# A graph layer by counts: the first layer's sum over edges as a product of an edge-count matrix and the node table, run in three stretches per block

## The reference, cut to what matters

```
t1    = feat @ W1
msg   = (t1[src] + feat[src] * feat[dst] @ W2) / (sqrt(deg[src]) * sqrt(deg[dst]))
agg   = segment_sum(msg, dst)
embed = l2_normalize(leaky_relu(t1 + agg + b))
```

## Time and profile before

| what | value |
|---|---|
| time, median of 3 runs | 5443.28 us (5443.25 to 5448.71) |
| profiled execution, span | 5537.5 us |
| mean granted TensorE clock | 0.835 of full |
| PE busy | 3805.9 us (69%) |
| DVE busy | 3132.6 us (57%) |
| ACT busy | 1618.8 us (29%) |
| POOL busy | 3849.2 us (70%) |
| DMA | 572.85 MB, mean 103 GB/s |

### The profile page before, as it was taken

One profiled execution on the slowest core, in us unless ns is written; L12 is line 12 of the kernel. 1 busy time (PEld: TensorE's weight loads), 2 busy tenths in 40 slices (PEclk: granted clock), 3 DMA queues, 4 the chain that ended last, 5 costly groups with the idle time before them and its releaser, 6 DMA issues.

```text
span 5537.5 us, 68744 instructions
## 1 busy us (share of the span) xinstructions
PE 3805.9 (69%) x19471; PEld 2905.8 (52%) x19471; DVE 3132.6 (57%) x12068; ACT 1618.8 (29%) x6417; POOL 3849.2 (70%) x4302
## 2 busy tenths in 40 slices
PE   6555555555556555555557887888788888888886
PEld 6444444444444444444445665656566666665654
DVE  8756565665655656555555555555455555555545
ACT  3144444544444444444420111111111111111111
POOL 0177776777777777776757777777777777777772
PEclk9577777777777777777779989999999998999988
DMA  4333333333333333333334444444444444444443
GB/s 97 117 94 97 93 99 92 99 94 98 98 97 96 96 98 93 96 95 94 95 104 116 113 111 111 113 115 112 110 115 110 115 114 110 111 110 114 112 108 76
DMA packets 278430, 572.85 MB, mean 103 GB/s; under 512 B 88622, under 2 KB 167790, under 8 KB 278056
## 3 DMA queue, kind: packets, MB, share of 16 engines
q0 software_dynamic: 164640, 456.82, 31.9%
q1 hardware_dynamic: 101576, 103.13, 6.9%
q10 hardware_dynamic: 11840, 8.50, 0.5%
HBM read 541.27 MB, written 26.92 MB: 103 GB/s over the span
## 4 chain that ended last, share of the span: by engine, by line
PE 42%; DVE 31%; another core or an unknown queue 16%; issue 9%; DMA 1%; ACT 0%; SPq 0%; DVEq 0%; PEldq 0%; ACTq 0%
PE psE L736 18%; DVE both L1366 8%; PE psY L717 6%; PE psT L717 6%; DVE work L1453 5%; DVE work L1449 4%; PE psE L936 3%; PE psE L917 3%; DVE work L1293 2%; PE psY L693 1%; DVE work L1383 1%; DMA acc_d<-work 1%; DVE work L1374 1%; PE psE L872 1%
## 5 line engine op out<-in xcount | busy, mean ns | idle before, releaser
L630 POOL DMA_INDIRECT work<-t_d,srci x3430 | 3271.3, 954 | 1587.8 <-issue 1155.8
L736 PE MATMUL psE<-work,both 128*128 128x257 f32 x6860 | 2219.4, 448 | 875.8 <-issue 373.7
L736 PEld LDWEIGHTS psE<-work,both 128*128 128x128 f32 x6860 | 1388.0, 225 | 1242.5 <-issue 469.2
L1109 ACT ACTIVATE work<-work 128x35 f16<-128x35 bf16 x5145 | 1133.5, 311 | 692.0 <-DVE work L1449 440.9
L1366 DVE TENSOR_SCALAR both<-iof,dstf 128x128 f32<-128x128 f32 x3430 | 813.7, 345 | 47.8 <-issue 25.7
L1449 DVE TENSOR_SCALAR work<-iob,work 128x35 bf16<-128x35 bf16 x1715 | 273.3, 269 | 806.4 <-remote 668.9
L1383 DVE TENSOR_TENSOR work<-work,psY 128x257 f32<-128x257 f32 x857 | 347.5, 420 | 631.1 <-PE psY L717 206.5
L1383 DVE TENSOR_TENSOR work<-work,psT 128x257 f32<-128x257 f32 x858 | 348.0, 420 | 601.1 <-PE psT L717 214.6
L717 PE MATMUL psT<-relb,work 126*128 126x257 bf16 x2574 | 452.1, 286 | 21.2 <-DVE work L1374 19.1
L717 PE MATMUL psY<-relb,work 126*128 126x257 bf16 x2577 | 459.8, 290 | 0.5 <-issue 0.5
L627 POOL MEMSET work<- 128x640 bf16 x571 | 380.2, 666 | 0.2
(11 more groups left out here) (262 smaller groups left out, 3291.1 us busy)
## 6 DMA issues: line engine op xcount, KB each, us to landing
work<-t_d,srci POOLq DMA_INDIRECT x3430
work<-types_d SPq DMA_DIRECT2D x245, 220.5 KB
both<-acc_d SPq DMA_DIRECT2D x98, 130.0 KB
t_d<-accf SPq DMA_DIRECT2D x7, 910.0 KB, 9.3
acc_d<-work ACTq DMA_DIRECT2D x1, 6370.0 KB
t_d<-accf SPq DMA_DIRECT2D x49, 130.0 KB
X<-in_x SPq DMA_DIRECT2D x1, 6144.0 KB
out<-X SPq DMA_DIRECT2D x6, 896.0 KB
```

Of the source, the lines that this page charges most:

```text
L630: pool.indirect_dma_start(gath[:, n % RG, :], None, table, bass.IndirectOffsetOnAxis(ap=srci[:, n:n + 1], axis=0)).then_inc(s_g[n % RG], 16)
L736: ins = nc.tensor.matmul(psE[:, b % 2, 0:DW], sel[:, third, k % SG, :], gath[:, n % RG, 0:DW], start=False, stop=(k == C - 1))
L1109: ins = nc.scalar.activation(to_s3[:, n % 2, i, j, :], to_s[:, n % 2, i, :], ACT.Copy, scale=load3[:, b // RB % 2, j, w:w + 1])
```

## The change

The first layer's sum no longer gathers rows. For each block of 128 targets it builds the matrix of edge counts, 6272 sources by 128 targets, and multiplies it with the whole table, which stays in SBUF as three bf16 parts that add up to the f32 value. In parts:

1. *Windows.* Each block is cut in 16 windows of 8 nodes (784 in all, `STEPS`). For each window SP loads 3x128 targets and sources at an address from a register (`windows`: 32 small transfers a block), ACT turns them to floats, TensorE transposes them (`turn_window`).
2. *One-hots.* For four windows at a time the Vector engine makes the one-hots with `tensor_tensor` over rows whose innermost run is four 16-bit values (`edge_hots`); `sends` is rewritten in the same form and takes over the scaling that ACT did.
3. *Histogram steps.* Each window is three bf16 products, 392, 294 and 147 columns wide, into one PSUM bank (two banks in turn), and ACT copies the 392 counts to bf16 (`counts_out`).
4. *Counts times table.* 49 sources x 3 parts = 147 bf16 products a block (`collect`), a block later, in three runs of 48, 48 and 51 at steps 5, 10 and 15.
5. *Start.* The table's three parts are made in SBUF; `t1_d` and a zeroed `acc_d` are still written for the fallback of unsorted inputs. X is loaded again block by block in the first pass, stored to `x1_d`, and all of it is loaded back at the start of the second pass, ahead of the third load of types. All seven `parts` now stand behind the last step.
6. GpSimd issues nothing in the first pass. The second pass is the same.

The fallback is taken where a block or window has more edges than its room. In the diff the loop over `range(STEPS + 50)` is TensorE's and the one over `range(STEPS + 55)` the Vector engine's; `at(t, lag)` gives the block whose step 0 lies `lag` steps back.

```diff
+NODES = 8
+WINS = P // NODES
+TAKE = 3
+REACH = ((0, 8), (2, 8), (5, 8))
+FOUR = 4
+STEPS = NB * WINS
...
+            def windows(b):
+                if b >= 2:
+                    sp.wait_ge(s_wtp, b - 1)
+                sp.load(firsts, start_w[0:1, WINS * b:WINS * b + WINS])
+                for w in range(WINS):
+                    first = sp.snap(firsts[w], min_val=0, max_val=E)
+                    for r, a in enumerate((dst_p, src_p)):
+                        sp.dma_start(ints[TAKE * w:TAKE * w + TAKE, b % 2, r, :],
+                                     a[bass.ds(first, ROOMY)].rearrange("(p e) -> p e", e=P)).then_inc(s_wl[b % 2], 16)
...
+            for b in range(NB + 3):
+                if b + 2 < NB:
+                    windows(b + 2)
+                if b >= 3:
+                    store_row(b - 3)
+                if b < NB:
+                    load_x(b)
                 if b + 1 < NB:
-                    load_old(0, b + 1)
+                    load_old0(b + 1)
...
+                for c in {NB - 1: (0, 1), NB: (2, 3), NB + 1: (4, 5), NB + 2: (6,)}.get(b, ()):
+                    load_pair(c)
...
+            load_types(0)
+            load_types(1)
+            for c in range(NB // 7):
+                sp.dma_start(X[:, 7 * c:7 * c + 7, :],
+                             x1_d.rearrange("(b p) d -> p b d", p=P)[:, 7 * c:7 * c + 7, :]).then_inc(s_xl, 16)
             sp.dma_start(f1, w1.rearrange("(t p) n -> p t n", p=P)).then_inc(s_fw, 16)
             sp.dma_start(f2, w2.rearrange("(t p) n -> p t n", p=P)).then_inc(s_fw, 16)
...
+            def histogram(t):
+                n, j = t // FOUR, t % FOUR
+                bank = (psT, psY)[t % 2][:, 1, :]
+                if j == 0:
+                    pe.wait_ge(s_r, n + 1)
+                if t >= 2:
+                    pe.wait_ge(s_a, t - 1)
+                for c, (lo, hi) in enumerate(REACH):
+                    ins = nc.tensor.matmul(bank[:, lo * NB:hi * NB], hot_l[n % 2][:, c, :, j],
+                                           hot_r[n % 2][:, AT[c]:AT[c + 1], j], start=(c == 0), stop=(c == TAKE - 1))
+                ins.then_inc(s_h, 1)
+
+            def collect(b, w):
...
+                for s in sources(w):
+                    for part, (at0, wide) in enumerate(((0, DW), (DW + 1, D), (DW + 1 + D, D))):
+                        ins = nc.tensor.matmul(bank[:, 0:wide], adj[:, b % 2, s, :], parts_t[:, s, at0:at0 + wide],
+                                               start=False, stop=(s == NB - 1 and part == 2))
...
+                for t in range(STEPS + 50):
+                    b, w = t // WINS, t % WINS
+                    if t < STEPS:
+                        histogram(t)
+                    if 1 <= b <= NB and w >= 1:
+                        collect(b - 1, w)
+                    if b + 1 < NB and w == 6:
+                        turn_window(b + 1)
+                    if b < NB and w in (4, 9, 14):
+                        move(b, w // 5)
...
+                    for m in at(t, 49):
                         feed_forward(m)
...
+                    for m in at(t, 46):
                         turn_ffn(m)
...
+                    for m in at(t, 37):
                         messages(m)
...
+                    for m in at(t, 35):
                         turn_features(m)
...
+            def counts_out(t):
+                b, w = t // WINS, t % WINS
+                if w == 0 and b >= 2:
+                    act.wait_ge(s_agg, b - 1)
+                act.wait_ge(s_h, t + 1)
+                bank = (psT, psY)[t % 2][:, 1, :]
+                nc.scalar.copy(adj[:, b % 2, :, NODES * w:NODES * w + NODES],
+                               bank[:, 0:NODES * NB].rearrange("p (d s) -> p s d", s=NB)).then_inc(s_a, 1)
...
+            def edge_hots(n):
+                b, j = n // FOUR, n % FOUR
+                if n >= 2:
+                    dve.wait_ge(s_h, FOUR * (n - 1))
+                mine = slice(FOUR * j, FOUR * j + FOUR)
+                for c, (lo, hi) in enumerate(REACH):
+                    many = (hi - lo) * NB
+                    v.tensor_tensor(hot_r[n % 2][:, AT[c]:AT[c + 1], :],
+                                    keyed_hi[:, b % 2, c, mine].unsqueeze(1).broadcast_to([P, many, FOUR]),
+                                    ramp[:, lo * NB:hi * NB, :], ALU.is_equal)
+                v.tensor_tensor(hot_l[n % 2][:, :, :, :],
+                                keyed_lo[:, b % 2, :, mine].unsqueeze(2).broadcast_to([P, TAKE, P, FOUR]),
+                                ramp[:, 0:P, :].unsqueeze(1).broadcast_to([P, TAKE, P, FOUR]), ALU.is_equal).then_inc(s_r, 1)
...
             def sends(b, g):                          # one third of a block: 12 columns
...
+                link(v.tensor_tensor(to_s, four(spot_s[:, r % 2, i, some]).broadcast_to([P, THIRDS, C, FOUR]), count(C),
+                                     ALU.is_equal))
+                for j in range(3):
+                    v.tensor_tensor(to_s3[:, n % 2, :, j, :, :], to_s,
+                                    four(load3[:, r % 2, j, i, some]).broadcast_to([P, THIRDS, C, FOUR]), ALU.mult)
+                v.tensor_tensor(to_q[:, n % 2, :, :, :], four(spot_q[:, r % 2, i, some]).broadcast_to([P, THIRDS, P, FOUR]),
+                                count(P), ALU.is_equal).then_inc(s_tq, 1)
...
+                for t in range(STEPS + 55):
+                    if t % FOUR == 0 and t // FOUR + 1 < BATCHES:
+                        edge_hots(t // FOUR + 1)
+                    if b < NB and w in (1, 6, 11):
+                        sends(b, w // 5)
...
+                    for m in at(t, 54):
+                        table_row(m)
+                    for m in at(t, 51):
+                        fed(m)
+                    for m in at(t, 45):
+                        ffn_input(m)
+                    for m in at(t, 42):
+                        residual(m)
+                    for m in at(t, 39):
+                        embeddings(m)
+                    for m in at(t, 33):
+                        features(m)
```

More of the change, by code:

```diff
@@ L34 @@
 RG = 18
-BURST = [6, 3]
+BURST = 3
+NODES = 8
+WINS = P // NODES
+TAKE = 3
+REACH = ((0, 8), (2, 8), (5, 8))
+ROOMY = TAKE * P
+FOUR = 4
+BATCHES = NB * WINS // FOUR
+STEPS = NB * WINS
+AT = [sum(hi - lo for lo, hi in REACH[:c]) * NB for c in range(TAKE + 1)]
+TW = 3 * D + 2
+XR = 3
+THIRDS = 3
+HALF = -(-NB // 2)
+TC4 = 12
+ENOUGH = ((2, 7.0), (5, 16.0), (8, 24.0))
+MOST = 16.0
 MM = 6
@@ new lines, in program @@
+        q = o - 8 * W
+        grown = arena[:, q:q + STEPS].rearrange("p (b u) -> p b u", u=WINS)
+        q += STEPS
+        ended = arena[:, q:q + NB]
+        q += NB
+        below = arena[:, q:q + NB]
+        q += NB
+        bands = arena[:, q:q + P].rearrange("p (k u) -> p k u", k=4)
+        q += P
+        offset = arena[:, q:q + WINS]
+        q += WINS
+        inside = arena[:, q:q + WINS]
+        q += WINS
+        under = arena[:, q:q + WINS]
+        q += WINS
+        over = arena[:, q:q + NB]
@@ L401, in program @@
         s_scaled = sem("s_scaled")
-        s_td = sem("s_td")
+        s_td = [sem(f"s_td{k}") for k in range(2)]
         s_sel = sem("s_sel")
@@ L568, in _ @@
+            sp.wait_ge(s_part, NB)
             unordered(0)
[L569 to L573 removed]
+            load_old0(0)
+            for b in range(NB + 3):
[5 more added lines that the diff above has]
+                    load_x(b)
@@ new lines, in rank_tri, with move @@
+            def rank_tri(b):
+                pe.wait_ge(s_pl, 2 * b + 1)
+                mine = marked[:, b % RB, :, :].rearrange("p c k -> p (c k)")
+                nc.tensor.matmul(psT[:, 0, 0:BINS * C], trib[:, :], mine, start=True, stop=True).then_inc(s_rp, 1)
+            def move(b, g):
+                n = THIRDS * b + g
+                pe.wait_ge(s_tq, n + 1)
+                if g == 0 and b >= 1:
+                    pe.wait_ge(s_so, b)
+                for k in third(g):
+                    i, t = k % TC4 // FOUR, k % FOUR
+                    ins = nc.tensor.matmul(psY[:, 0, 0:3 * C], to_q[:, n % 2, i, :, t], to_s3[:, n % 2, i, :, :, t],
+                                           start=(k == 0), stop=(k == C - 1))
+                ins.then_inc(s_sm, 1)
@@ L1083, in _ @@
[L1083 to L1096 removed]
+            act.wait_ge(s_padd, 64)
@@ new lines, in _ @@
+            for n in range(EN):
+                if n >= 2:
+                    dve.wait_ge(s_hmm, n - 1)
+                for one_hot, bits, wide in ((ohlo, end_lo, P), (ohhi, end_hi, NB)):
+                    ins = v.tensor_tensor(one_hot[:, n % 2, :, :],
+                                          bits[:, HG * n:HG * n + HG].unsqueeze(1).broadcast_to([NP, wide, HG]),
+                                          counted[:, 0:wide, :], ALU.is_equal)
+                ins.then_inc(s_oh, 1)
+            link(v.memset(cnt[:, :], 0.0))
```

991 lines of the change are left out of this document (608 added, 383 removed).

## The result

The kernel after takes 4898.01 us (median of 4 runs, 4891.59 to 4907.67), where the kernel before took 5443.26 beside it: a ratio of 0.9002, 95% interval 0.8989 to 0.9015, 545 us less. The forecast was 4817, with a range of 4600 to 5140. Its profiled execution has a span of 4905.9 us at a mean granted clock of 0.932.

What follows compares the result with a forecast made beforehand. A loop of DVE and PE lags, no single engine, was to bound the first pass: 317 + 49 x 37.5 - 18 = 2136, tail 50, second pass at 2186 (-649), net -637, scaled -626: 4817 us, range 4600 to 5140.

Steps and rivals of the forecast that it cites:

- cost of the reload behind it: Start of second pass: 6.4 MB of X loaded ahead of the third types takes 19 us, of which 12 counted.
- No engine alone sets the block: First pass: lags tie DVE and PE in turn, giving 37.5 us a block; likeliest case, 35 to 40 us, chance 0.52.
- I take 0.35, for ACT hides part of it (next), and keep 3.7 for the range: Histogram step on PE: 0.35 us; strided operands could make it 0.58, adding 3.7 us a block.
- PE's 29.8: TensorE's work per block in the new first pass: 29.8 us together, or 59 at the low clock.
- a loop of lags, 35.5: First-pass block: stretches of PE and DVE waiting on each other sum to 35.2 us, with semaphores 35.5.
- 2 us of allowance: Added to the first-pass block: one for pieces at the low clock, one for lumps such as `marks` and `in_place`.
- the rival of full cover: First pass: DVE's 33.3 us alone sets the block; time 4615 us, chance 0.15.
- lumps of work: First pass, `marks` and `in_place` every third block: 1 us a block allowed.
- The rival in which it falls between runs: First pass: clock drops between product runs, PE's 29.8 becomes 45, block 44 us; time 5130 us, chance 0.21.
- scaled the gain by the ratio of the two, 0.983: Whole kernel: profiled execution ran 1.7% above the median, so -637 on its span became -626 on 5443.3.

Runs made afterwards that it cites:

- the pairs version: Kernel after with source one-hots laid out by pairs of edges, so the moving operand lies 4 bytes apart instead of 8, counts right: 4779.24 us, ratio 0.8642.
- the version with one run: Kernel after with a block's 147 products in one run at the last histogram step in place of three runs: 5219.1 us.
- the kernel after on the second chip: Kernel after, unchanged, on another chip, where the kernel before took 5529.93 us: 4941.04 us, ratio 0.8938.
- versions with the same second pass: Kernel after with one-hots in pairs, plus either products spread over all 15 steps (4621.27 us) or the moves in pairs too (4683.32 us).
- the version that stands for it: Kernel after with only the histogram products' weights taken from consecutive values, counts wrong, on the fast chip: 4793.27 us.

## Why the prediction was right, and where it was off

*Each term against the trace.*

| step of the prediction | forecast | measured |
|---|---|---|
| one-hot forms on DVE | 969, 764, 457, 952 ns | 974, 764, 459, 953 |
| ACT's copy of 392 counts | 0.48 us | 0.486 |
| product of counts and table | 0.113 us | 0.113 |
| a histogram step on PE | 0.35 (0.58 or 0.6 in the range) | 0.74 |
| a move | 0.06 to 0.08 us | 0.10 |
| PE, DVE busy in the pass | 0.8, 0.85 | 0.97, 0.76 |
| DVE's work in a block | 33.3 us | 29.3 |
| block | 37.5 us | 38.7 (37.2, 37.2, 41.6) |
| step 0 starts | 317 | 295.7 |
| last step ends | 2136 | 2158.9 |
| tail to the first gather | 50 us | 56.6 |
| gather point | 2186 | 2215.6 |
| cost of the reload behind it | 12 us | 19.4 |

*What bounds the block.* "No engine alone sets the block" was wrong. TensorE does, in two blocks of three without any standing and in the third but for 2.5 us, and the error sits in one term: "I take 0.35, for ACT hides part of it (next), and keep 3.7 for the range." The bound at 0.58 us a step was taken from weight loads with a gap of 60 bytes at 0.70 ns a column; a moving operand 8 bytes apart costs 0.83 to 0.84 ns at the full clock. It costs 16 x 0.39 = 6.2 us a block more than the 5.6 of the forecast, and the moves 1.1 more than their 2.4. Added to PE's 29.8 that is 37.1, and the blocks take 37.2. That the 37.5 came out close is luck: the forecast got there by a loop of lags, 35.5, and 2 us of allowance, and TensorE's sum, which it put at 29.8 and so held to be no bound, was short by 7.3, which brings it to nearly the same figure. The experiments with the moving operand alone, the weights alone and less DVE work show it: 163, 0 and 3 us at the gather point. The Trainium skill (SBUF — State Buffer, Door 1: The DMA port swizzle) was cited for full rate at two operands in a 16-byte line, "by it the 3.7 falls away". The runs speak against it for TensorE's moving operand: 8 bytes apart ran at half the rate, 4 bytes apart at the full one.

*DVE.* Its one-hots cost what was forecast, its old tasks less. The forecast took the work that goes from one group of seven slots, 18.7 us a block. Over 1000 to 2000 us of the kernel before, the same three lines (L1366, L1449, L1453) are busy 402.8 us, 21.0 a block. The `parts` leave the pass too. It bound nothing here, but it makes the rival of full cover, DVE alone at 33.3, too high by 4.

*The loop.* Its 35.5 stood right behind: with PE's columns at full rate a block of the pairs version takes 32.9 us twice and 40.0 the third time, 35.3 on average, and the waits are those that the forecast named, PE at `turn_ffn` (42.1 us from 1000 to 1900 us) and DVE before `embeddings` (24.3). This loop is most of why the moving operand's rate gave 163 us and not the 280 that it took from PE. For lumps of work, such as `marks` and `in_place` in every third block, the forecast had 1 us; in the kernel after they cost 4.4 in the third block, 1.5 on average. PE stands there 2.5 us for `ffn_input`. In the stretches of that block it is first busy 3.83 and 3.65 us of 5, and in the second of these and the one behind it the clock is 0.77 and 0.92:

```profile
1378.00:1383.00 5.00, 5.00 (x44) 4.16 (x43) 4.64 (x15) 0.00 (x0) 0.00 (x0) 1.00 0.09 27
1383.00:1388.00 5.00, 3.83 (x23) 2.29 (x21) 4.64 (x9) 2.05 (x5) 0.00 (x0) 1.00 0.00 0
1388.00:1393.00 5.00, 3.65 (x19) 2.58 (x20) 3.59 (x8) 0.92 (x3) 0.00 (x0) 0.77 0.00 0
1393.00:1400.00 7.00, 7.00 (x50) 5.37 (x48) 3.65 (x9) 0.97 (x2) 0.00 (x0) 0.92 0.01 2
```

*The clock.* The rival in which it falls between runs didn't come true; histogram steps and runs both ran under 0.98. It did come true in part in the version with one run, where PE paused.

*The ends.* The start was 21 us shorter than forecast, the 49 blocks 44 longer (1863 against 1819), the tail 7 longer. At the tail PE stands 7.4 us for DVE, which then works on the last block's order tasks. With these moved, that stand is gone from the trace, but PE then waits 5.9 us for `features` and 5.9 for `ffn_input`, and the gather point gains only 2 us: the chain of the last block sets the tail. The third types come late behind the reload, as the forecast feared. DVE waits 22.6 us for them, and the wait (DVE, the same line of the kernel after on the second chip)

```profile
2259.95 0.58 DVE L1745 TENSOR_SCALAR arena<-arena,tid 126x640 bf16<-126x640 f16 x2 [22.63 <-DMA arena<-types_d]
```

is not covered by the gathers that run ahead: they stop after 24 slots and stand 19.7 us (the row shown with the seam). That is the 19.4 us lost behind the gather point on one chip; in the kernel before no gather waits over 2.4 us there.

*From the span to the time.* On the chip of both traces, 5540.4 and 4946.5, the change takes 594 us; the forecast was 637. The missing 43 are 29 for the later gather point (2215.0 there, forecast 2186), 7 for that of before, which lies at 2828.3 there, and 7 for the reload. The timed difference is 545. The last 49 are, as far as the totals tell, no property of the kernel after: the profiled execution of before took what all its runs take on a chip with slower gathers than the timed ones. I had scaled the gain by the ratio of the two, 0.983, which takes away 11. But what such a chip adds lies in the gathers: behind the gather point the kernel after takes 2731.5 us on it, and versions with the same second pass 2671.7 and 2680.0 on a chip where the kernel before takes 5444. Half of the gathers of before are in the pass that the change removes. So half of the 94 us between its profiled and its timed executions, 47, was to come off the gain: 5443 - 590 = 4853. With the 43 of the terms above that is 4896, where 4898 was measured. No trace of the kernel before was taken on the chip of its timed runs, so the even split of the 94 is not shown. The totals bear it out between these two kinds of chip: the kernel before takes 87 us more on the slower one (5529.9 against 5443.3), the kernel after 43. It is no rule: on the fast chip the kernel before gains 289 us on its 5443, and the kernel after, by the version that stands for it, 105. So of the 81 us by which the forecast was too low, 43 are its terms, 36 a scaling that took off 11 where 47 had to go, and 2 are left over.

## What to carry to other kernels

Give a layout that one engine writes a price on the engine that reads it: values 8 bytes apart were free for VectorE to write, and cost TensorE twice the time to stream; runs of two values served both. Put long runs of products on TensorE as short pieces between the steps that other engines wait for, for one run of 16.5 us cost 5.7 us a block, and 15 pieces of about 1.1 us gave back 2.4 a block against three of 5.5. And when a profiled execution and the median differ, ask which stage holds the difference before scaling a gain by it.

## What the runs showed of the hardware

- A bf16 moving operand streams at 0.44 ns a column from consecutive values, at 0.45 ns 4 bytes apart and at 0.84 ns 8 bytes apart, all at a granted clock of 0.97 to 0.98. Weight loads of 128 columns took 117 to 120 ns 8 bytes apart (118 in the moves), 98 ns 4 bytes apart (in the moves), and 107 to 111 with the histogram's weights consecutive.
- VectorE's comparison of 16-bit values keeps its rate when the innermost run is two values: 1568 elements in 977 ns, against 974 with runs of four.
- Chips differ in the pace of the pass with gathers, and in nothing else seen here. From 3000 to 4000 us, on the chips where the kernel before takes 5530 and 5155, the kernel after (first row) and the version with the weights close (second row, the same second pass) issue 656 and 697 gathers. One takes GpSimd 947 and 946 ns by the median, but on the slower chip it stands 47 us until TensorE frees a slot, on the other 8.7. What is slower behind that, the traces don't show.

```profile
L816 POOL DMA_INDIRECT arena<-t_d,srci x656: 942/947/1072, 3000.4 to 3998.9; - x164
```

```profile
L818 POOL DMA_INDIRECT arena<-t_d,srci x697: 942/946/1081, 3000.1 to 3999.4; - x175
```
